# 16 bit comparisons on VectorE in a graph kernel: a 16 bit number table in PSUM, one-hots laid out number by number, selection matrices in two halves

## The chip, the cores and the metric

The kernel runs on 1 core of one Trainium2 chip. A core has five engines with queues of their own: TensorE (PE; its weight loads are listed apart as PEld), VectorE (DVE), ScalarE (ACT), GpSimd (POOL) and SyncE (SP), and 16 DMA engines. The metric is the device time in microseconds (us); of the kernel before, three runs were timed.

## What is computed

There are 12500 nodes with 64 numbers each and 212500 edges, sorted by their destination `dst`. Two graph layers follow each other, cut here to what matters:

```python
def _L0_gnn_ref(node_feats, edge_feats, src, dst, W1, b1, W2, b2, gamma, beta):
    msg = node_feats[src] + edge_feats
    agg = jax.ops.segment_sum(msg, dst, num_segments=n_nodes)
    h = jax.nn.relu(agg @ W1 + b1) @ W2 + b2
    ...                                   # batch norm over the nodes

def _L1_gnn_ref(x, edges, W1, b1, W2, b2, ln_w, ln_b):
    # two of: xw[src] * enorm[:, None], summed by dst, + b, relu; then one norm over everything
    ...
h = jnp.maximum(_layernorm(x), 0.0); x = x + _L0_gnn_ref(h, edge_attr_64, ...)
h = jnp.maximum(_layernorm(x), 0.0); x = x + _L1_gnn_ref(h, edge_index, ...)
```

So there are three passes over the edges (pass 0 for the first layer, passes 1 and 2 for the second), each a gather of rows by `src` and a sum by `dst`.

## The kernel before

A pass sums the edges in two ways. The edges of the lowest destinations are summed by **count matrices** ("dense windows"): for a window of 125 destinations, a matrix of 12500 sources by 125 destinations says how many edges lie between each pair, and TensorE multiplies it by the node table, in 100 matmuls of 125x125 times 125x193 (`app`, line 1110). Pass 0 has 54 such windows, passes 1 and 2 have 69. The rest of the edges come in **groups** of 1280 edges (128 partitions of NT=10 edges) and one small last group: POOL gathers the source rows from DRAM with one indirect DMA for each of the 10 edges of a partition (`pool_gather`, line 1273), and TensorE adds them up by destination with 10 matmuls whose weights are a **selection matrix** S, 128 edges by W=96 destinations, one for each of the 10 (`grp`, line 1132). In pass 0 all 167 groups also bring their edge features from DRAM; these take the same selection matrices (line 1125), and 79 of the groups are gathered besides. In passes 1 and 2 there are 54 gathered groups each.

The count matrices are themselves built on TensorE, in pass 0 for its 54 windows and in pass 1 for 17 more, and are kept in DRAM for the passes behind. One matrix takes 25 matmuls (`bld`, line 1089) of 128 edges each. Their weights are **one-hots** of a source's number within its block of 125 (VectorE, `ob`, line 958: five of them by one instruction of 5x125 elements, so NB4=5), and their moving operand is a one-hot of the block, times 1 or 256 for two destinations in one (VectorE, `oh`, line 961, 300 elements). ScalarE packs the counts out of PSUM (line 1211).

A one-hot is a comparison of a number with a row of numbers 0, 1, 2, ... Line 958 compares `modT` (16 bit) with `ps_i`, a table of 128 numbers in PSUM in fp32. Line 971 makes a whole selection matrix, 10x96 elements, by comparing `relT` (16 bit, edge's destination less the group's first) with the same table. Both results are 16 bit in SBUF, in rows of 125 or 96 destinations that lie side by side, and TensorE loads one such row in each partition as weights.

VectorE also splits the edge features of pass 0 into three bf16 parts (line 987, two subtractions of 650 fp32 elements per group, both inputs and the output in SBUF), folds the sums (lines 994, 1004) and adds them into `acc` (lines 1022, 1027).

The order of work on PE, ACT, DVE and SP is a list that `make_plan` writes: every item gets a due time in units of four `app` matmuls, and each engine runs its items by due time; a build's one-hots are due 3.3 units before its matmul, a group's S 7 units before its matmuls. The rings are short: NOH=6 `oh` buffers, NOB=3 `ob` buffers (15 one-hots), NS=2 selection matrices, NEDGE=2 buffers of edge features, NSLOT=4 groups of gathered rows. POOL runs the gathers in order, and a gather waits only until the group four before has been used. Before pass 0 stands a first part (layer norm, tables, the lists by run of edges), in which `dve_late_constants` (line 567) makes small constants.

Of the kernel before, what the change touches and what calls it, by code (L numbers as in the profile page):

```python
# [5 lines left out]
ALU = mybir.AluOpType  # L6
# [7 lines left out]
U8 = mybir.dt.uint8  # L14
# [3 lines left out]
P = 128  # L18
# [166 lines left out]
def bass_gnn_preln_kernel(nc, x, src, dst, edge, W01, b01, W02, b02, gamma, beta,  # L185
# [32 lines left out]
    with ExitStack() as ctx:  # L218
# [47 lines left out]
        relT = sb("relT", [P, NT, G], F16)  # L266
# [43 lines left out]
        ps_i = psum[:, 2, 0:P]  # L310
        ps_t = [psum[:, i, :] for i in range(2)]
# [34 lines left out]
        def sbuf(n):  # L346
            return part(o_S, n, NT * W // 2).bitcast(BF16).rearrange("p (t w) -> p t w", w=W)
# [165 lines left out]
        def sp_load():  # L513
            sp.dma_start(run_first, row_first).then_inc(l_first, 16)
            sp.dma_start(dst_i, dst_turned.rearrange("p t g -> p (t g)")).then_inc(l_dst, 16)
# [51 lines left out]
        def dve_late_constants():  # L567
# [4 lines left out]
            dve.tensor_copy(identb[:, :], ident[:, :]).then_inc(v_ident, 1)  # L572
            bound, late, limit = run_f[:, 0, :], run_f[:, 3, :], run_f[:, 2, :]
# [153 lines left out]
        def dve_lists():  # L727
            dve.wait_ge(l_dst, 2 * 16)
            firsts = base_b[:, 0:G].rearrange("p (a g) -> p a g", a=1).broadcast_to([P, NT, G])
            dve.tensor_tensor(relT[:, :, :], dst_i.rearrange("p (t g) -> p t g", g=G), firsts, ALU.subtract).then_inc(  # L730
                v_list, 1)
            dve.wait_ge(l_small, N_SMALL)
            V(dve.tensor_copy(rel_l[0:R, 0:2], dst_l[0:R, :]))
            V(dve.tensor_copy(rel_l[0:R, 4:5], dstb_l[0:R, :]))
            V(dve.tensor_scalar(rel_l[0:R, 2:4], rel_l[0:R, 0:2], rel_l[0:R, 4:5], None, ALU.subtract))
            dve.tensor_copy(relh_l[0:R, :], rel_l[0:R, 2:4]).then_inc(v_list, 1)

        def dve_check_lists():
            every = relT.rearrange("p t g -> p (t g)")
# [205 lines left out]
        def dve_pass(k, early=None):  # L945
            pl = plans[k]
            fe = FE if k == 0 else F
            for kind, v in half(pl, "dve", early):
                if kind == "oh":
                    if k == 1 and v == pl["b"]:  # L950
                        dve.wait_ge(st_x1, NCH * NBAND * 16)
                    if v % NB4 == 0:
# [10 lines left out]
                elif kind == "S":  # L963
# [4 lines left out]
                    if g < G:  # L968
                        rel = relT[:, :, g:g + 1].broadcast_to([P, NT, W])
                        it = ps_i[:, 0:W].rearrange("p (a w) -> p a w", a=1).broadcast_to([P, NT, W])  # L970
                        dve.scalar_tensor_tensor(out=S, in0=rel, scalar=0.0, in1=it, op0=ALU.add,  # L971
                                                 op1=ALU.is_equal).then_inc(v_S, 1)
                    else:
                        rel = relh_l[0:R, :].rearrange("p (t a) -> p t a", a=1).broadcast_to([R, 2, W])
                        it = ps_i[0:R, 0:W].rearrange("p (a w) -> p a w", a=1).broadcast_to([R, 2, W])
                        dve.scalar_tensor_tensor(out=S[0:R, 0:2, :], in0=rel, scalar=0.0, in1=it, op0=ALU.add,
                                                 op1=ALU.is_equal).then_inc(v_S, 1)
# [97 lines left out]
        def pe_pass(k, early=None):  # L1075
# [3 lines left out]
            for kind, v in half(pl, "pe", early):  # L1079
                if kind == "bld":  # L1080
# [8 lines left out]
                    pe.matmul(to[:, :, 2 * side:2 * side + 3], ob(v // NB4 % NOB)[:, v % NB4, :],  # L1089
# [24 lines left out]
                elif kind == "grp":  # L1114
# [7 lines left out]
                    if k == 0:  # L1122
                        pe.wait_ge(v_rest2, v + 1)
                        for t in range(nt):
                            last = pe.matmul(ps_q, S[0:parts, t, :], e3(v % NEDGE)[0:parts, t, :, :],  # L1125
                                             start=(t == 0), stop=(t == nt - 1 and not gathered))
                    if gathered:
# [3 lines left out]
                        for t in range(nt):  # L1131
                            last = pe.matmul(to, S[0:parts, t, :],  # L1132
# [252 lines left out]
        def slow_group(k, g, parts, nt):  # L1385
# [35 lines left out]
            gb, S = gbuf(0), sbuf(0)  # L1421
# [578 lines left out]
```

## Time and profile before

| | us |
|---|---|
| median of three runs | 2910.58 (2907.73 to 2920.95) |
| the profiled execution | 2908.32 |
| its span | 2906.8 |

Of the span PE is busy for 2552.8 us (88%), its weight loads for 2416.9 (83%), POOL for 1993.7 (69%), DVE for 1743.1 (60%) and ACT for 888.7 (31%). The granted clock of TensorE was 0.956 of full speed on the mean. "Busy" of PE counts from the start to the modelled end of matmuls that overlap, so it is no measure of how near PE is to its limit. The first part lasts to about 107 us, pass 0 to about 1337, the norms between the layers to about 1410, pass 1 to about 2180 and pass 2 to about 2900.

### The profile page before, as it was taken

The page shows a single profiled execution, that of the slowest core. Times are in us where ns is not written, and L with a number is a line of the kernel's source. Part 1 is how long each engine was busy: PE and PEld are TensorE (multiplying, and loading weights), DVE is VectorE, ACT ScalarE, POOL GpSimd, SP SyncE. Part 2 cuts the span into 40 slices and gives each one's busy share as a digit, 9 for nine tenths or more (in the row PEclk, how much of TensorE's full clock was granted, in tenths as well). Part 3 has the DMA queues.
Part 4 walks back from the last instruction along what each step waited for, and adds up shares of the span by engine and source line. Part 5 has one row for each costly group of instructions (what it writes and reads, how often), then busy time and mean ns, then how long its engine had stood idle before and what let it go on. Part 6 is the DMA issues. An engine that isn't in the chain of part 4 may idle for free.

```text
span 2906.8 us, 64340 instructions
## 1 busy us (share of the span) xinstructions
PE 2552.8 (88%) x25984; PEld 2416.9 (83%) x25984; DVE 1743.1 (60%) x4148; ACT 888.7 (31%) x1492; POOL 1993.7 (69%) x1903
## 2 busy tenths in 40 slices
PE   0388988989888898895699999999997999999996
PEld 0277878878787787784699999999997999999996
DVE  8898999989988899895444444454430222222222
ACT  7344444444444444454522222232210000000001
POOL 6777777777777778710377777767706777777772
PEclk9899999999999999996799999999998999999998
DMA  4455565555556555543765555655557666666664
GB/s 116 118 149 144 147 171 151 155 157 153 148 160 153 150 148 168 148 125 105 231 204 201 163 200 196 211 181 179 200 186 203 221 206 214 208 213 199 199 214 131
DMA packets 341214, 503.37 MB, mean 173 GB/s; under 512 B 278659, under 2 KB 284217, under 8 KB 316082
## 3 DMA queue, kind: packets, MB, share of 16 engines
q1 hardware_dynamic: 280102, 402.60, 42.8%
q0 software_dynamic: 60192, 93.34, 14.0%
q8 instruction: 214, 3.51, 0.5%
q10 hardware_dynamic: 616, 3.20, 0.4%
q14 instruction: 90, 0.73, 0.1%
HBM read 361.86 MB, written 137.13 MB: 172 GB/s over the span
## 4 chain that ended last, share of the span: by engine, by line
PE 42%; POOL 37%; issue 11%; DVE 5%; DMA 2%; ACT 1%; SPq 1%; DVEq 0%; ACTq 0%; POOLq 0%
POOL arena L1273 37%; PE psum L1110 32%; PE psum L1089 3%; PE psum L1132 3%; PE psum L1071 1%; DMA arena<-table,srcT 1%; ACT arena L818 1%; DMA arena<-in_edge_attr_dram 1%; SPq L1288 0%; PE psum L1125 0%; PE psum L1195 0%; DMA arena<-table 0%; DVE arena L961 0%; DVE arena L834 0%; DVE arena L844 0%
## 5 line engine op out<-in xcount | busy, mean ns | idle before, releaser
L1273 POOL DMA_INDIRECT arena<-table,srcT x1840 | 1913.0, 1040 | 696.3 <-issue 626.5
L1110 PE MATMUL psum<-arena 125*125 125x193 bf16 (+1 forms) x19200 | 2009.1, 250 | 44.8 <-DMA arena<-counts 23.0
L1110 PEld LDWEIGHTS psum<-arena 125*125 125x125 fp8e4 x19200 | 1879.1, 140 | 87.1 <-DMA arena<-counts 23.5
L1211 ACT CAST arena<-psum 125x500 uint16<-125x500 f32 (+1 forms) x923 | 647.3, 711 | 1084.3 <-PE psum L1089 1079.8
L1089 PE MATMUL psum<-arena 128*125 128x300 f16 x1775 | 609.9, 346 | 31.6 <-DVE arena L961 24.5
L961 DVE TENSOR_SCALAR arena<-iota,keyT,oddT 128x300 f16<-128x300 f16 x1775 | 579.3, 353 | 1.4 <-PE psum L1089 1.3
L1089 PEld LDWEIGHTS psum<-arena 128*125 128x125 f16 x1775 | 247.8, 140 | 79.5 <-DVE arena L961 58.4
L971 DVE SCALAR_TENSOR_TENSOR arena<-relT,psum 128x960 bf16<-128x960 f16 x272 | 308.6, 1134 | 0.0
L987 DVE TENSOR_TENSOR arena<-arena 128x650 f32<-128x650 f32 (+1 forms) x334 | 272.8, 817 | 24.8 <-DMA arena<-in_edge_attr_dram 24.6
L958 DVE TENSOR_TENSOR arena<-modT,psum 128x625 f16<-128x625 f16 x355 | 281.0, 792 | 0.2 <-issue 0.2
L994 DVE TENSOR_REDUCE arena<-psum 96x65 f32<-96x195 f32 (+1 forms) x275 | 96.3, 350 | 307.4 <-PE psum L1132 303.4
L1132 PE MATMUL psum<-arena 128*96 128x192 bf16 x1846 | 201.0, 258 | 59.2 <-DMA arena<-table,srcT 59.2
L1132 PEld LDWEIGHTS psum<-arena 128*96 128x96 bf16 x1846 | 174.9, 130 | 65.6 <-DMA arena<-table,srcT 54.8
L1255 ACT ACTIVATE cneg<-cst 125x1 f32<-125x1 f32 x25 | 5.1, 203 | 685.4 <-DVE arena L1046 685.4
L1004 DVE TENSOR_REDUCE arena<-psum 125x64 f32<-125x192 f32 x192 | 67.1, 349 | 234.0 <-PE psum L1110 233.8
L1125 PE MATMUL psum<-arena 128*96 128x195 bf16 (+1 forms) x1662 | 189.5, 262 | 2.4 <-DVE arena L987 2.4
L1022 DVE SCALAR_TENSOR_TENSOR acc<-psum,acc 65x96 f32 (+1 forms) x275 | 67.3, 245 | 194.4 <-PE psum L1191 161.1
L1125 PEld LDWEIGHTS psum<-arena 128*96 128x96 bf16 (+1 forms) x1662 | 166.6, 128 | 5.2 <-issue 3.9
L1027 DVE SCALAR_TENSOR_TENSOR acc<-psum,acc 64x125 f32<-64x125 f32 x192 | 53.3, 278 | 105.5 <-PE psum L1195 96.1
L1003 DVE COPY cnt<-psum 125x1 f32<-125x1 f32 x123 | 18.7, 152 | 154.3 <-PE psum L1110 153.9
L1643 POOL TENSOR_TENSOR arena<-arena 125x1600 f32<-125x1600 f32 x3 | 8.6, 2867 | 132.9 <-DVE arena L1633 132.9
L1191 PE MATMUL psum<-ident,arena 96*65 96x96 f32 (+1 forms) x275 | 70.5, 256 | 29.5 <-DVE acc L1027 27.1
(219 smaller groups left out, 954.2 us busy)
## 6 DMA issues: line engine op xcount, KB each, us to landing
arena<-counts SPq DMA_DIRECT2D x121, 1600.0 KB
counts<-arena SPq DMA_DIRECT2D x71, 1600.0 KB, 6.1
arena<-in_edge_attr_dram SPq DMA_DIRECT2D x166, 320.0 KB
arena<-table,srcT POOLq DMA_INDIRECT x1840
table<-arena SPq DMA_DIRECT2D x8, 1050.0 KB
table<-arena SPq DMA_DIRECT2D x25, 168.0 KB
arena<-table SPq DMA_DIRECT2D x4, 1050.0 KB
arena<-in_x_dram ACTq DMA_DIRECT2D x4, 700.0 KB
```

The source lines that it names most:

```text
L958: dve.tensor_tensor(ob(four % NOB), mod, it, ALU.is_equal)
L961: dve.tensor_scalar(oh(v % NOH), iota1[:, :], keyT[:, v:v + 1], oddT[:, v:v + 1], ALU.is_equal, ALU.mult).then_inc(v_oh, 1)
L971: dve.scalar_tensor_tensor(out=S, in0=rel, scalar=0.0, in1=it, op0=ALU.add, op1=ALU.is_equal).then_inc(v_S, 1)
L987: dve.tensor_tensor(ebuf(e, i + 1)[0:parts, 0:nt * FE], a, upper, ALU.subtract).then_inc(v_rest1 if i == 0 else v_rest2, 1)
L994: dve.tensor_reduce(qbuf(n % 2)[:, 0:fe], ps_q.rearrange("p (s f) -> p f s", s=3)[:, 0:fe, :], X, ALU.add).then_inc(v_fq, 1)
L1089: pe.matmul(to[:, :, 2 * side:2 * side + 3], ob(v // NB4 % NOB)[:, v % NB4, :], oh(v % NOH).rearrange("p (j m) -> p j m", m=3), start=(sid ...
L1110: last = pe.matmul(ps_v[n % 2][0:PN, 0:xc], A(slot)[0:PN, j, 0:PN], Xs[0:PN, j, 0:xc], start=(j == 0), stop=(j == J - 1))
L1125: last = pe.matmul(ps_q, S[0:parts, t, :], e3(v % NEDGE)[0:parts, t, :, :], start=(t == 0), stop=(t == nt - 1 and not gathered))
L1132: last = pe.matmul(to, S[0:parts, t, :], gbuf(slot)[0:parts, t, :].rearrange("p (s f) -> p s f", s=3), start=(k > 0 and t == 0), stop=(t = ...
L1191: pe.transpose(ps_g[0:fe, 0:W], qbuf(m % 2)[:, 0:fe], ident[0:W, 0:W]).then_inc(p_win, 1)
L1211: act.copy(A2(slot)[0:PN, :, i // 2 * NWORD:i // 2 * NWORD + n_w], ps_b[at % NBANK][0:PN, :].rearrange("p (j x) -> p j x", x=NWORD)[:, :, ...
L1273: pool.indirect_dma_start(out=gbuf(slot)[0:parts, t, :], out_offset=None, in_=tables[k], in_offset=bass.IndirectOffsetOnAxis(ap=idx, axis= ...
```

## The change

What it does:

- `num_dn` is a new table in PSUM, in fp16: element (d, n) holds d, for d from 0 to 124 and n from 0 to 4, so each number stands five times side by side. It is written once, by three new instructions in `dve_late_constants`: a memset of 313 words, a cast of 625 elements from the fp32 `iota`, and a copy of the 313 words into PSUM.
- Line 958's instruction stays one `tensor_tensor` of 625 elements. Its inputs are now `modT` (rows of 5 numbers, read again for each d) and `num_dn`, and its output lies as (d, n), so all three operands are 16 bit with a step of one element in the innermost dimension, where before `modT` stood still for 125 elements and the table was fp32.
- Line 971's one `scalar_tensor_tensor` of 960 elements becomes two `tensor_tensor` of 480 elements, for the edges 0 to 4 and 5 to 9 of each partition. S lies as (w, t); `relT` is turned to (g, t) for it, and with it the list that the host lays out.
- TensorE's weights are therefore no longer side by side: a one-hot of `ob` is read in steps of 5 elements (10 bytes), a selection matrix of S in steps of 10 elements (20 bytes). The matmuls, their number and sizes stay.

```diff
+        n_num = (PN * NB4 + 1) // 2
+        ps_n5 = psum[:, 2, P:P + n_num]
+        num_dn = ps_n5.bitcast(F16)[:, 0:PN * NB4].rearrange("p (d n) -> p d n", n=NB4)
...
         def ob(k):
 
-            return part(o_ob, k, n_ob).bitcast(F16)[:, 0:NB4 * PN].rearrange("p (n d) -> p n d", d=PN)
+            return part(o_ob, k, n_ob).bitcast(F16)[:, 0:NB4 * PN].rearrange("p (d n) -> p d n", n=NB4)
...
         def sbuf(n):
+            return part(o_S, n, NT * W // 2).bitcast(BF16).rearrange("p (w t) -> p w t", t=NT)
...
             dve.tensor_copy(identb[:, :], ident[:, :]).then_inc(v_ident, 1)
+            nums = arena[:, o_t + NE + 16:o_t + NE + 16 + n_num]
+            V(dve.memset(nums, 0.0))
+            V(dve.tensor_copy(nums.bitcast(F16)[:, 0:PN * NB4].rearrange("p (d n) -> p d n", n=NB4),
+                              iota[:, 0:PN].rearrange("p (d a) -> p d a", a=1).broadcast_to([P, PN, NB4])))
+            V(dve.tensor_copy(ps_n5, nums))
...
-                        mod = modT[:, v:v + NB4].rearrange("p (n a) -> p n a", a=1).broadcast_to([P, NB4, PN])
-                        it = ps_i[:, 0:PN].rearrange("p (a d) -> p a d", a=1).broadcast_to([P, NB4, PN])
-                        dve.tensor_tensor(ob(four % NOB), mod, it, ALU.is_equal)
+                        mod = modT[:, v:v + NB4].rearrange("p (a n) -> p a n", a=1).broadcast_to([P, PN, NB4])
+                        dve.tensor_tensor(ob(four % NOB), mod, num_dn, ALU.is_equal)
...
-                        rel = relT[:, :, g:g + 1].broadcast_to([P, NT, W])
-                        it = ps_i[:, 0:W].rearrange("p (a w) -> p a w", a=1).broadcast_to([P, NT, W])
-                        dve.scalar_tensor_tensor(out=S, in0=rel, scalar=0.0, in1=it, op0=ALU.add,
-                                                 op1=ALU.is_equal).then_inc(v_S, 1)
+                        for t0 in (0, NB4):
+                            rel = relT[:, g:g + 1, t0:t0 + NB4].broadcast_to([P, W, NB4])
+                            last = dve.tensor_tensor(S[:, :, t0:t0 + NB4], rel, num_dn[:, 0:W, :], ALU.is_equal)
+                        last.then_inc(v_S, 1)
...
-                    pe.matmul(to[:, :, 2 * side:2 * side + 3], ob(v // NB4 % NOB)[:, v % NB4, :],
+                    pe.matmul(to[:, :, 2 * side:2 * side + 3], ob(v // NB4 % NOB)[:, :, v % NB4],
...
-                            last = pe.matmul(ps_q, S[0:parts, t, :], e3(v % NEDGE)[0:parts, t, :, :],
+                            last = pe.matmul(ps_q, S[0:parts, :, t], e3(v % NEDGE)[0:parts, t, :, :],
...
-                            last = pe.matmul(to, S[0:parts, t, :],
+                            last = pe.matmul(to, S[0:parts, :, t],
```

The instructions' order stays on PE, ACT, POOL and SP. On DVE two places differ. The first is in the first part of the program, behind the constants (L572 writes the bf16 identity, L574 and L575 start the bounds of the edge runs); before and after:

```order
L571 TENSOR_SCALAR ident<-arena,rowf 128x128
L572 CAST identb<-ident 128x128
L574 TENSOR_SCALAR arena<-arena 128x14
L575 SCALAR_TENSOR_TENSOR arena<-arena 128x14
L577 TENSOR_SCALAR arena<-arena 128x14
```

```order
L577 TENSOR_SCALAR ident<-arena,rowf 128x128
L578 CAST identb<-ident 128x128
L580 MEMSET arena 128x313
L581 CAST arena<-arena 128x625
L583 COPY psum<-arena 128x313
L585 TENSOR_SCALAR arena<-arena 128x14
L586 SCALAR_TENSOR_TENSOR arena<-arena 128x14
L588 TENSOR_SCALAR arena<-arena 128x14
```

Three instructions have come in ahead of the bounds. The second place stands for every group, here one in pass 0, on DVE again; the lines are 958 and 968 for `ob`, 961 and 971 for `oh`, 971 and 981 for S, 987 and 995 for the edge features, before and after:

```order
L958 TENSOR_TENSOR arena<-modT,psum 128x625
L961 TENSOR_SCALAR arena<-iota,keyT,oddT 128x300
L1003 COPY cnt<-psum 125x1
L1004 TENSOR_REDUCE arena<-psum 125x64
L971 SCALAR_TENSOR_TENSOR arena<-relT,psum 128x960
L961 TENSOR_SCALAR arena<-iota,keyT,oddT 128x300
L994 TENSOR_REDUCE arena<-psum 96x65
L961 TENSOR_SCALAR arena<-iota,keyT,oddT 128x300
L987 TENSOR_TENSOR arena<-arena 128x650
```

```order
L968 TENSOR_TENSOR arena<-modT,psum 128x625
L971 TENSOR_SCALAR arena<-iota,keyT,oddT 128x300
L1011 COPY cnt<-psum 125x1
L1012 TENSOR_REDUCE arena<-psum 125x64
L981 TENSOR_TENSOR arena<-relT,psum 128x96x5 x2
L971 TENSOR_SCALAR arena<-iota,keyT,oddT 128x300
L1002 TENSOR_REDUCE arena<-psum 96x65
L971 TENSOR_SCALAR arena<-iota,keyT,oddT 128x300
L995 TENSOR_TENSOR arena<-arena 128x650
```

The selection matrix has become two instructions in the same place; nothing else has moved.

## Rows read from the trace of the kernel before

**Rows 1.** The page: chain of waits by engine, then by line, shares of the span.

```profile
PE 42%; POOL 37%; issue 11%; DVE 5%; DMA 2%; ACT 1%; SPq 1%; DVEq 0%; ACTq 0%; POOLq 0%
```

**Rows 2.** Busy time by stretch: PE, PEld, DVE, ACT, POOL, then clock, DMA.

```profile
110.00:1250.00 1140.00, 1000.60 (x8889) 899.07 (x8887) 1029.15 (x2456) 506.38 (x792) 900.69 (x780) 0.95 0.57 153
1255.00:1337.00 82.00, 71.47 (x591) 59.30 (x588) 60.62 (x147) 32.21 (x58) 0.00 (x0) 0.90 0.52 140
1420.00:2170.00 750.00, 747.48 (x8211) 736.69 (x8210) 341.79 (x947) 204.35 (x309) 513.30 (x532) 1.00 0.58 197
2210.00:2900.00 690.00, 663.41 (x7706) 659.23 (x7704) 151.09 (x366) 27.21 (x81) 488.66 (x518) 0.98 0.61 201
```

**Rows 3.** POOL's groups in pass 0: count, busy us, mean ns, idle before.

```profile
L1273 POOL DMA_INDIRECT arena<-table,srcT x778 | 898.9, 1155 | 237.1 <-issue 236.2 <-PE psum L1125 0.6 <-PE psum L1132 0.3
```

**Rows 4.** The same of POOL in pass 2, 2210 to 2900 us.

```profile
L1273 POOL DMA_INDIRECT arena<-table,srcT x516 | 486.9, 944 | 157.3 <-issue 157.0 <-PE psum L1132 0.3
```

**Rows 5.** DVE's and PE's groups in pass 0, 110 to 1250 us.

```profile
L961 DVE TENSOR_SCALAR arena<-iota,keyT,oddT 128x300 f16<-128x300 f16 x1278 | 418.0, 353 | 1.4 <-PE psum L1089 1.3
L987 DVE TENSOR_TENSOR arena<-arena 128x650 f32<-128x650 f32 x310 | 254.1, 820 | 21.6 <-DMA arena<-in_edge_attr_dram 21.6
L958 DVE TENSOR_TENSOR arena<-modT,psum 128x625 f16<-128x625 f16 x256 | 202.6, 791 | 0.0
L971 DVE SCALAR_TENSOR_TENSOR arena<-relT,psum 128x960 bf16<-128x960 f16 x156 | 176.7, 1133 | 0.0
...
L1089 PE MATMUL psum<-arena 128*125 128x300 f16 x1278 | 443.3, 349 | 27.3 <-DVE arena L961 20.4 <-ACT arena L1211 4.0 <-issue 0.2
L1132 PE MATMUL psum<-arena 128*96 128x192 bf16 x780 | 90.6, 269 | 49.8 <-DMA arena<-table,srcT 49.8
```

**Rows 6.** The timeline of POOL and DVE: start us, length us, what.

```profile
616.79 0.82 DVE L987 TENSOR_TENSOR arena<-arena 128x650 f32<-128x650 f32 x1
616.82 1.61 POOL L1273 DMA_INDIRECT arena<-table,srcT  x1 [0.30 <-issue]
617.80 0.82 DVE L987 TENSOR_TENSOR arena<-arena 128x650 f32<-128x650 f32 x1
...
621.03 1.14 DVE L971 SCALAR_TENSOR_TENSOR arena<-relT,psum 128x960 bf16<-128x960 f16 x1
621.70 0.94 POOL L1273 DMA_INDIRECT arena<-table,srcT  x1 [0.30 <-issue]
622.10 0.35 DVE L961 TENSOR_SCALAR arena<-iota,keyT,oddT 128x300 f16<-128x300 f16 x1
```

**Rows 7.** The chain in order of time, pieces: start us, us, what.

```profile
18.27 0.18 DVE arena L575
106.84 1.05 POOL arena L1273
1241.52 0.92 PE psum L1125 x10
1248.03 0.85 PE psum L1132 x10
1509.76 5.11 PE psum L1110 x60
1515.65 0.85 PE psum L1071 x8
```

**Rows 8.** The last gather of pass 0, and a 16 bit DVE operation, in the timeline.

```profile
1247.18 0.89 POOL L1273 DMA_INDIRECT arena<-table,src_l  x1 [0.30 <-issue]
...
15.52 2.00 DVE L602 TENSOR_SCALAR arena<-arena 128x1792 bf16<-128x1792 f16 x3
```

**Rows 9.** DVE's and PE's groups in the tail of pass 0, 1255 to 1337 us.

```profile
L971 DVE SCALAR_TENSOR_TENSOR arena<-relT,psum 128x960 bf16<-128x960 f16 x10 | 11.4, 1140 | 0.0
L958 DVE TENSOR_TENSOR arena<-modT,psum 128x625 f16<-128x625 f16 x12 | 9.5, 792 | 0.0
L1145 PE MATMUL psum<-acc,w 64*128 64x500 f32 x8 | 5.3, 753 | 4.0 <-DVE acc L1022 4.0
```

More of the change, by code:

```diff
@@ L13 @@
 U16 = mybir.dt.uint16
-U8 = mybir.dt.uint8
 X = mybir.AxisListType.X
@@ L265, in bass_gnn_preln_kernel @@
         srcT = sb("srcT", [P, NT, G - G0], I32)
-        relT = sb("relT", [P, NT, G], F16)
+        relT = sb("relT", [P, G, NT], F16)
         keyT = sb("keyT", [P, NBLD + NBLD % 2], F16)
@@ L310, in bass_gnn_preln_kernel @@
         ps_i = psum[:, 2, 0:P]
+        n_num = (PN * NB4 + 1) // 2
+        ps_n5 = psum[:, 2, P:P + n_num]
+        num_dn = ps_n5.bitcast(F16)[:, 0:PN * NB4].rearrange("p (d n) -> p d n", n=NB4)
+        assert NT == 2 * NB4
         ps_t = [psum[:, i, :] for i in range(2)]
@@ L346, in sbuf, with sbuf_rows @@
         def sbuf(n):
+            return part(o_S, n, NT * W // 2).bitcast(BF16).rearrange("p (w t) -> p w t", t=NT)
+        def sbuf_rows(n):
             return part(o_S, n, NT * W // 2).bitcast(BF16).rearrange("p (t w) -> p t w", w=W)
@@ L514, in sp_load @@
             sp.dma_start(run_first, row_first).then_inc(l_first, 16)
-            sp.dma_start(dst_i, dst_turned.rearrange("p t g -> p (t g)")).then_inc(l_dst, 16)
+            sp.dma_start(dst_i, dst_turned.rearrange("p g t -> p (g t)")).then_inc(l_dst, 16)
             sp.dma_start(base_b, group_first.broadcast_to([P, NG])).then_inc(l_dst, 16)
@@ L728, in dve_lists @@
             dve.wait_ge(l_dst, 2 * 16)
-            firsts = base_b[:, 0:G].rearrange("p (a g) -> p a g", a=1).broadcast_to([P, NT, G])
-            dve.tensor_tensor(relT[:, :, :], dst_i.rearrange("p (t g) -> p t g", g=G), firsts, ALU.subtract).then_inc(
+            firsts = base_b[:, 0:G].rearrange("p (g a) -> p g a", a=1).broadcast_to([P, G, NT])
+            dve.tensor_tensor(relT[:, :, :], dst_i.rearrange("p (g t) -> p g t", t=NT), firsts, ALU.subtract).then_inc(
                 v_list, 1)
@@ L738, in dve_check_lists @@
         def dve_check_lists():
-            every = relT.rearrange("p t g -> p (t g)")
+            every = relT.rearrange("p g t -> p (g t)")
             dve.wait_ge(v_list, 2)
@@ L968, in dve_pass @@
                     if g < G:
-                        rel = relT[:, :, g:g + 1].broadcast_to([P, NT, W])
-                        it = ps_i[:, 0:W].rearrange("p (a w) -> p a w", a=1).broadcast_to([P, NT, W])
-                        dve.scalar_tensor_tensor(out=S, in0=rel, scalar=0.0, in1=it, op0=ALU.add,
-                                                 op1=ALU.is_equal).then_inc(v_S, 1)
-                    else:
[L974 to L977, printed above, removed]
+                        for t0 in (0, NB4):
+                            rel = relT[:, g:g + 1, t0:t0 + NB4].broadcast_to([P, W, NB4])
+                            last = dve.tensor_tensor(S[:, :, t0:t0 + NB4], rel, num_dn[:, 0:W, :], ALU.is_equal)
+                        last.then_inc(v_S, 1)
+                    else:
+                        rel = relh_l[0:R, :].rearrange("p (a t) -> p a t", a=1).broadcast_to([R, W, 2])
+                        dve.tensor_tensor(S[0:R, :, 0:2], rel, num_dn[0:R, 0:W, 0:2], ALU.is_equal).then_inc(v_S, 1)
                 elif kind in ("rest1", "rest2"):
@@ L1420, in slow_group @@
             pool.sem_clear(t_idx)
-            gb, S = gbuf(0), sbuf(0)
+            gb, S = gbuf(0), sbuf_rows(0)
             for t in range(nt):
@@ L1982 @@
     laid['x'] = x.reshape(-1, PN, F).transpose(1, 0, 2).reshape(PN, -1)
-    for name, a in (('src_turned', src), ('dst_turned', dst)):
-        laid[name] = a[0:n_groups * P * NT].reshape(n_groups, P, NT).transpose(1, 2, 0)
+    for name, a, order in (('src_turned', src, (1, 2, 0)), ('dst_turned', dst, (1, 0, 2))):
+        laid[name] = a[0:n_groups * P * NT].reshape(n_groups, P, NT).transpose(*order)
     behind = _np.stack([_np.full(P, n_nodes, dst.dtype), _np.zeros(P, dst.dtype)], axis=1)
```

## The prediction, before the changed kernel ran

> **What bounds the kernel now.** The change touches VectorE (DVE) and the layout of TensorE's (PE's) weights, so I first ask who sets the end in each stage. The page's chain of waits gives PE 42%, POOL 37% and DVE 5% [rows 1]. The table by stretch says where [rows 2]. From 110 to 1250 us (pass 0) three engines look full: DVE 1029 of 1140 us, PE 1001, POOL 901. In pass 1 (1420 to 2170) PE is busy for 747 of 750 us and DVE for 342; in pass 2 (2210 to 2900) PE for 663 of 690, DVE for 151. So passes 1 and 2 are PE's, and no saving on DVE can shorten them.
>
> In pass 0 the busy share misleads. POOL's group has 237.1 us of idle time in front of 778 gathers, and 236.2 of it is "issue", 0.30 us ahead of each; for the matmuls that free its four slots it waits 0.9 us in all [rows 3]. POOL thus starts each gather as soon as the one before has ended, without a break: from 106.84 to 1247.18 + 0.89 = 1248.1 us [rows 7, 8] is 1141 us for 782 gathers, 1.46 us each. As it never waits for DVE or PE, a faster DVE gives it nothing. The others show the other side: PE waits 49.8 us for gathered rows and 27.3 us ahead of line 1089, of which 20.4 for one-hots [rows 5]. DVE is the second slowest; it falls behind and catches up within the four groups that the slots allow.
>
> Can DVE slow POOL in another way? A gather takes 1155 ns on the mean in pass 0 and 944 in pass 2 [rows 3, 4], so 778 x 0.211 = 164 us of pass 0 is stretch. The timeline says with which DVE work: the gather at 616.82 takes 1.61 us beside two of line 987 (fp32, both inputs in SBUF, 0.82 us each), the one at 621.70, whose first half lies beside line 971, takes 0.94 [rows 6]. Those that stretch it are line 987 and, less, line 961; the change touches neither, and their number stays.
>
> **The change part by part.**
>
> *Line 958, 355 instructions (270 for pass 0, 85 for pass 1).* 625 elements take 791 ns, line 971's 960 take 1133 [rows 5]: (1133 - 791) / 335 = 1.02 ns per element, and 0.15 us fixed, of which 0.07 lies beside the next instruction (971 starts at 621.03, is 1.14 long, the next starts at 622.10 [rows 6]). The trace has no two-input 16 bit operation with all operands packed. Bounds: 1.04 ns per element as now; from below line 602's one-input 16 bit operation, 3 of 1792 elements in 2.00 us [rows 8], some 0.35 ns. I take half of the present rate, 0.52 ns: two numbers a step is what 16 bits beside 32 suggests, and line 961 (300 elements in 353 ns, (0.353 - 0.15) / 300 = 0.68 [rows 5]) lies between. Saved: 625 x 0.5 = 0.32 us each.
>
> *Line 971, 272 instructions (166 for pass 0).* Now 1.06 us from start to start; then 2 x (0.07 + 480 x 0.52) = 0.64, so 0.43 us saved. At the present rate it would be 2 x (0.07 + 0.50) = 1.14, 0.08 more.
>
> DVE's work in pass 0 falls by 270 x 0.32 + 166 x 0.43 = 158 us (bounds: 13 more; 208 less), in pass 1 by 50 and in pass 2 by 23. In pass 0 nothing of it reaches the end while POOL runs: it becomes DVE waiting for gathers. Value 0, bounds -15 to +15 us, for the stretch of the gathers may shift as DVE's gaps do.
>
> At this place the Trainium skill disagrees with itself. Its page "VectorE: DVE Perf Modes" (the perf-mode tier table) gives `tensor_tensor` one element per cycle as soon as an operand is in PSUM; "Vector Engine (DVE) Microarchitecture Reference" (5.1, performance modes) lets it take two with one source in PSUM, also for rows of odd length such as these 5. No row here decides it. By the first DVE saves nothing, by the second what I took; the sum is the same but for the tail.
>
> *The tail of pass 0, 1255 to 1337 us.* POOL is idle there and DVE is busy for 61 of 82 us, PE for 71 [rows 2]. DVE has 10 of line 971 and 12 of line 958 in it [rows 9]: 10 x 0.43 + 12 x 0.32 = 8.1 us saved. PE is nearly full, so only its gaps can close: 82 - 71.5 = 10.5 us, of which 4.0 wait for sums that DVE adds [rows 9], and some for DMA. Value -5, bounds -8 to 0.
>
> *The head.* Three DVE instructions come in on the chain, which runs through line 575 at 18.27 us [rows 7]. The memset and the copy have 313 elements, the cast 625; at 1.02 ns and 0.15 fixed, each waiting for the one before: 0.47 + 0.79 + 0.47 = 1.7; at half the rate 1.1. Value +1.5, and the first gather at 106.84 goes with it.
>
> *The weight loads.* This is where the change can cost. All loads of the trace read columns side by side. An `app` matmul with its load takes 5.11 / 60 = 85 ns, a selection matmul 0.85 / 10 = 85 [rows 7]: 192 or 193 columns set this, the loads hide behind them. How long may a load take before it shows? Line 1071 loads 125 four-byte columns and moves only 64: 0.85 / 8 = 106 ns a pair [rows 7], so the load sets it, at 0.85 ns per column. If a strided 2-byte column is no slower than that four-byte one, a selection matrix (96 columns) takes 82 ns: hidden. A one-hot (125 columns) takes 106, 21 more than the matmul ahead: 425 in pass 1, 9 us at most; its step of 10 bytes is the smaller one, so I take 3. Bounds 0 and, if a strided column takes twice a four-byte one (1.7 ns), the rival below.
>
> *Nothing else.* relT, its copy from DRAM and its subtraction keep their sizes; no queue gets another DMA and no engine another wait.
>
> **Sum** against the profiled execution (2908.3; its span is 2906.8): +1.5 - 5 + 3 = -0.5. The runs' median lies 2.3 above that execution, so the forecast is 2910 in terms of the median, own range 2896 to 2924: no change that a measurement tells (about 0.5%, 15 us).
>
> **The rivals.**
>
> *A, slower: strided weights load slower than the matmul ahead.* For it: the load is barely hidden (82 of 85 ns even at the four-byte rate), and moving columns that step by 4 bytes (line 1125) already take 0.92 per 10 against 0.85 [rows 7], 3 columns more but 7 ns, not 1. Against: those 7 ns are little. It decides from 85 ns a load, 0.85 ns per column. At 1.7 ns a selection load takes 163 ns, +78 for each: in passes 1 and 2, where PE has no slack, 1064 x 78 = 83 us, and 425 one-hots with, say, +60 make 26. In pass 0, 2440 x 78 + 1350 x 60 = 271 us against PE's idle 1140 - 1001 = 139 [rows 2]: +132. Together +241, 3150 us; at 1.05 ns per column, (101 - 85) x 1064 and 46 x 425 make +37 with pass 0 absorbed, 2947.
> The Trainium skill names such a mechanism: "SBUF — State Buffer" (specifications, and its note on cachelines) says that SBUF is read in 16-byte lines, that full rate needs at least two hits in a line, and that each access that crosses to a new line pays. It gives no figure. In S every column would be in another line, in `ob` five of eight. No load here has such a step; line 1125's four columns to a line, nearly at full rate, do not contradict it.
>
> *B, faster: gathers stretch less.* If DVE is no longer full, gaps fall between lines 987 and 961, and POOL gets in. Against: the stretch goes with the count of those two. A quarter of 164 us gone gives 2869.
>
> *C, faster: DVE is the bound of pass 0 after all.* Its waits on PE and full 1029 us speak for it, POOL's 0.9 us against. All 158 us off, until PE's 1001 us stop it: -139, 2771.
>
> *D, the 16 bit rate does not come.* DVE +13 us in pass 0, hidden; 10 x 0.08 us in the tail instead of -5: 2916, no change.
>
> **How the numbers follow.** The forecast 0.43, D 0.09, A 0.26 (a third of it near 2947, the rest above 2960), B 0.16, C 0.04, and 0.02 for what I don't see. Faster: B, C and a little of the forecast, 0.22; slower: A and a little of the forecast, 0.28; within 0.5%: 0.50. The range for 8 in 10 reaches over most of B and the cheap part of A: 2872 to 2965; above it is the dear part of A.
>
> **What would show it.** Right: line 968 at about 475 ns and line 981 at about 400; POOL's issue still without waits in pass 0, 1.46 us per gather; PE's waits for gathered rows grown from 49.8 us to over 100; `app` and selection matmuls still 85 ns a pair in pass 2; the first gather 1 to 2 us later. Wrong: selection matmuls at 100 ns or more a pair in passes 1 and 2 (A); gathers of pass 0 under 1100 ns on the mean (B); POOL's last gather of pass 0 long before 1240 us (B or C); lines 968 and 981 at 790 and 650 ns (D).

## The result, and the profile after

The changed kernel takes 3090.35 us (median of four runs, 3087.82 to 3091.70); the kernel before, timed again beside it, 2914.76 (2907.73 to 2920.95). The ratio is 1.0602, with a 95% interval of 1.0573 to 1.0631: 175.6 us, or 6%, slower. I had forecast 2910 and a range up to 2965. Rival A, the strided weight loads, is what happened; the range reached only over its cheap part.

The page's chain of waits of the changed kernel, by engine, shares of the span, beside [rows 1]:

```profile
PE 84%; DVE 6%; DMA 4%; ACT 2%; issue 1%; SPq 1%; POOL 1%; DVEq 1%; ACTq 0%; POOLq 0%
```

POOL has fallen from 37% to 1% and PE has doubled. The stretches of the changed kernel that answer to [rows 2], with the same columns (us, PE, PEld, DVE, ACT, POOL, granted clock, DMA share, GB/s):

```profile
110.00:1290.00 1180.00, 1144.19 (x8547) 1069.79 (x8548) 924.59 (x2520) 491.12 (x761) 856.22 (x780) 0.99 0.54 144
1300.00:1420.00 120.00, 117.01 (x894) 106.51 (x894) 87.62 (x241) 46.45 (x78) 0.00 (x0) 0.99 0.46 134
1510.00:2330.00 820.00, 818.10 (x8263) 807.45 (x8260) 316.24 (x1003) 204.86 (x309) 511.48 (x531) 1.00 0.54 180
2350.00:3060.00 710.00, 697.49 (x7665) 694.70 (x7666) 138.79 (x397) 18.49 (x69) 499.23 (x530) 0.99 0.62 198
```

In pass 0 PE now has 36 us without work where it had 139, and its granted clock is 0.99 where it was 0.95: it has few pauses left. The reader's first sign of the cause is that PE does the same 25,984 matmuls in more time. The groups of weight loads over the whole span, their forms apart (count, busy us, mean ns, idle before), of the kernel before:

```profile
L1089 PEld LDWEIGHTS psum<-arena 128*125 128x125 f16 x1775 | 247.8, 140 | 79.5 <-DVE arena L961 58.4 <-issue 18.9
L1132 PEld LDWEIGHTS psum<-arena 128*96 128x96 bf16 x1840 | 174.4, 130 | 65.3 <-DMA arena<-table,srcT 54.8 <-issue 10.3
```

and of the changed kernel:

```profile
L1097 PEld LDWEIGHTS psum<-arena 128*125 128x125 f16 x1775 | 391.8, 221 | 49.5 <-DVE arena L971 31.7 <-issue 17.2
L1140 PEld LDWEIGHTS psum<-arena 128*96 128x96 bf16 x1840 | 323.1, 260 | 9.4 <-DMA arena<-table,srcT 9.4
```

A selection matrix's load has gone from 130 to 260 ns and a one-hot's from 140 to 221, with the same columns and bytes. The chain of the changed kernel in pass 0 (start us, us, what) shows what that does to a pair of load and matmul; it answers to [rows 7]:

```profile
606.38 1.68 PE psum L1133 x10
608.06 1.67 PE psum L1140 x10
```

That is 167 to 168 ns a pair, where before it was 85 (line 1132) and 92 (line 1125). From start to start of the records, a one-hot's pair (line 1097, which moves 300 elements) takes 211 ns for 156.

POOL in pass 0 of the changed kernel answers to [rows 3], and PE's two groups to [rows 5]:

```profile
L1281 POOL DMA_INDIRECT arena<-table,srcT x779 | 854.9, 1097 | 320.0 <-issue 222.5 <-PE psum L1140 97.5
```

```profile
L1097 PE MATMUL psum<-arena 128*125 128x300 f16 x1232 | 483.2, 395 | 11.9 <-DVE arena L971 8.8 <-ACT arena L1219 0.5
L1140 PE MATMUL psum<-arena 128*96 128x192 bf16 x750 | 137.5, 333 | 9.0 <-DMA arena<-table,srcT 9.0
```

The roles are swapped. POOL waits 97.5 us for PE to free its slots (0.9 before), and PE waits 9.0 us for gathered rows (49.8 before) and 11.9 ahead of the one-hot matmuls (27.3 before). The mean gather of 1097 ns is under the 1100 that I had named as a sign of rival B; here it stands in a slower kernel, so that sign was no good by itself.

**Where the time is.** Between the two medians lie 175.6 us, between the spans of the two traces 182.5. The stages, from the start of their first to the start of their last instruction, in us:

| | before | after | difference |
|---|---|---|---|
| first gather of pass 0 | 106.8 | 108.8 | +1.9 |
| pass 0, first gather to the norms | 1234.8 | 1321.5 | +86.7 |
| pass 1, first to last `app` matmul | 765.4 | 831.4 | +66.0 |
| pass 2, first to last `app` matmul | 698.4 | 725.6 | +27.2 |

The differences add to 182 of the 182.5 us. In pass 1 they are the loads and nothing else: 532 selection pairs x 82 ns and 425 one-hots x 55 ns make 67. In pass 0, 782 pairs of line 1140 x 82, 1662 of line 1133 x 76 and 1350 one-hots x 55 are 265 us more work for PE, of which 178 did not lengthen the pass. Of the 87 that did, 42 lie before POOL's last gather (1183 us of gathers for 1141) and 45 behind it (139 us for 94), where PE works off what it is late with. In pass 2, 532 x 82 = 44 gave 27.

**VectorE.** Not all comparisons got as fast as expected. The changed kernel's groups over the whole span, forms apart:

```profile
L981 DVE TENSOR_TENSOR arena<-relT,psum 128x480 bf16<-128x480 f16 x544 | 298.6, 633 | 0.0
L968 DVE TENSOR_TENSOR arena<-modT,psum 128x625 f16<-128x625 f16 x355 | 189.3, 533 | 0.1
```

A block of one-hots went from 791 to 533 ns (I took 475), but each half of a selection matrix took 633 (I took 400). With 0.15 us fixed that is 0.61 ns per element for the first and 1.00, the old rate, for the second. VectorE's busy time from the first gather to the norms fell from 1099 to 1026 us, by 73 where I had 158.

### The profile page after: what moved, and what is told of

Read it like the earlier page. It is cut to its first block, busy times and chain, and to the rows that moved or that the text cites. A ratio compares the mean times of both kernels' runs of the same rounds, so it can differ in the third digit from the quotient of the medians.

```text
span 3089.3 us, 64615 instructions
## 1 busy us (share of the span) xinstructions
PE 2853.4 (92%) x25984; PEld 2744.4 (89%) x25984; DVE 1641.6 (53%) x4423; ACT 891.2 (29%) x1492; POOL 1945.9 (63%) x1903
## 4 chain that ended last, share of the span: by engine, by line
PE 84%; DVE 6%; DMA 4%; ACT 2%; issue 1%; SPq 1%; POOL 1%; DVEq 1%; ACTq 0%; POOLq 0%
PE psum L1118 49%; PE psum L1097 11%; PE psum L1140 10%; PE psum L1133 8%; DMA arena<-in_edge_attr_dram 3%; PE psum L1079 1%; DVE arena L995 1%; PE psum L1153 1%; PE psum L1156 1%; PE psum L1199 1%; PE psum L1203 1%; DVE arena L971 1%; POOL arena L1281 1%; ACT arena L829 1%; DVEq L1028 0%
## 5 line engine op out<-in xcount | busy, mean ns | idle before, releaser
L1281 POOL DMA_INDIRECT arena<-table,srcT x1840 | 1867.3, 1015 | 843.7 <-issue 610.0
L1097 PE MATMUL psum<-arena 128*125 128x300 f16 x1775 | 695.1, 394 | 12.2 <-DVE arena L971 8.8
L1097 PEld LDWEIGHTS psum<-arena 128*125 128x125 f16 x1775 | 391.8, 221 | 49.5 <-DVE arena L971 31.7
L1140 PE MATMUL psum<-arena 128*96 128x192 bf16 x1846 | 338.1, 332 | 9.0 <-DMA arena<-table,srcT 9.0
L1140 PEld LDWEIGHTS psum<-arena 128*96 128x96 bf16 x1846 | 324.4, 260 | 9.7 <-DMA arena<-table,srcT 9.4
L1133 PE MATMUL psum<-arena 128*96 128x195 bf16 (+1 forms) x1662 | 304.3, 330 | 0.3 <-DVE arena L995 0.3
L981 DVE TENSOR_TENSOR arena<-relT,psum 128x480 bf16<-128x480 f16 x544 | 298.6, 633 | 0.0
L1133 PEld LDWEIGHTS psum<-arena 128*96 128x96 bf16 (+1 forms) x1662 | 292.2, 260 | 1.4 <-issue 1.2
L968 DVE TENSOR_TENSOR arena<-modT,psum 128x625 f16<-128x625 f16 x355 | 189.3, 533 | 0.1
```

The source lines that it names most:

```text
L968: dve.tensor_tensor(ob(four % NOB), mod, num_dn, ALU.is_equal)
L981: last = dve.tensor_tensor(S[:, :, t0:t0 + NB4], rel, num_dn[:, 0:W, :], ALU.is_equal)
L1133: last = pe.matmul(ps_q, S[0:parts, :, t], e3(v % NEDGE)[0:parts, t, :, :], start=(t == 0), stop=(t == nt - 1 and not gathered))
L1140: last = pe.matmul(to, S[0:parts, :, t], gbuf(slot)[0:parts, t, :].rearrange("p (s f) -> p s f", s=3), start=(k > 0 and t == 0), stop=(t = ...
L1281: pool.indirect_dma_start(out=gbuf(slot)[0:parts, t, :], out_offset=None, in_=tables[k], in_offset=bass.IndirectOffsetOnAxis(ap=idx, axis= ...
```

## The experiments

Each kernel was timed in three rounds beside the kernel before on the same chip, unless it says otherwise. Diffs are against the changed kernel where not told, and each shows only the lines that matter.

**One part alone: one-hots changed, selection matrices as before.**

```diff
-                    S = sbuf(n % NS)
+                    S = sbuf_rows(n % NS)
-                            last = pe.matmul(to, S[0:parts, :, t],
+                            last = pe.matmul(to, S[0:parts, t, :],
```

(and S written by one `scalar_tensor_tensor` again).

> The changed kernel with its selection matrices as before: one instruction, one row of 96 destinations per edge, read side by side; one-hots stay 16 bit and strided (10 bytes). Theory L (strided weight loads set the time; in the changed kernel's trace a selection matmul with its load takes 167 ns for 85, a one-hot's matmul 211 for 156): only 1775 x 55 = 98 us of TensorE work is left, 425 of them (23 us) in pass 1 without slack, 74 us in pass 0 against 139 us of idle, most of it absorbed; 2940 to 2955 us. Theory D (the time comes from VectorE: new reads of PSUM, two instructions for a selection matrix, later results): the half of the cost that belongs to the selection matrices goes too, but the matmul pairs stay slow; 3000 or so.

2915.29 us (2908.14 to 2919.56), ratio 0.9998, interval 0.9983 to 1.0014: no change, below what I expected. Pass 1 is 22 us longer (787.5 for 765.4, 425 x 55 = 23), and the gathers of pass 0 are 13 us shorter (1128.4 for 1141.2, 1139 ns on the mean for 1155). So in pass 1 the strided one-hots cost what the arithmetic says, and the shorter gathers of pass 0 give about as much back.

**The other part alone: selection matrices changed, one-hots as before.**

```diff
-                        dve.tensor_tensor(ob(four % NOB), mod, num_dn, ALU.is_equal)
+                        it = ps_i[:, 0:PN].rearrange("p (a d) -> p a d", a=1).broadcast_to([P, NB4, PN])
+                        dve.tensor_tensor(ob(four % NOB), mod, it, ALU.is_equal)
-                    pe.matmul(to[:, :, 2 * side:2 * side + 3], ob(v // NB4 % NOB)[:, :, v % NB4],
+                    pe.matmul(to[:, :, 2 * side:2 * side + 3], ob(v // NB4 % NOB)[:, v % NB4, :],
```

> The changed kernel with its one-hots (line 958 of before) as before; selection matrices stay in two halves and strided by 20 bytes. Theory L: 1064 x 82 = 87 us in passes 1 and 2, and in pass 0 1662 x 76 + 782 x 82 = 190 us against 139 of idle, +51 or a little more; 3050 to 3070 us. With e1 the two parts should add up to more than the whole in passes 1 and 2 alone, and to less than it in pass 0, where each can use the idle time by itself. Theory D: as e1, 3000 or so.

3033.34 us (3028.65 to 3037.94), ratio 1.0404, interval 1.0366 to 1.0441, or +120 us. That is below the 3050 to 3070 expected; the selection matrices are still the larger part. Alone the two cost 2 and 120, together 176. Pass 1 adds up: +22 and +43 alone, +66 together. Pass 0, from the first gather on, does not: -14 and +52 alone, +87 together. Each alone can use PE's pauses; together they have used them up.

**The strides alone: VectorE slow as before, its results laid out as after.**

```diff
-                        dve.tensor_tensor(ob(four % NOB), mod, num_dn, ALU.is_equal)
+                        it = ps_i[:, 0:PN].rearrange("p (d a) -> p d a", a=1).broadcast_to([P, PN, NB4])
+                        dve.tensor_tensor(ob(four % NOB), mod, it, ALU.is_equal)
```

(S likewise, by one `scalar_tensor_tensor` of 960 elements.)

> Only the layout: results laid out and loaded as in the changed kernel, but compared with the fp32 table, one instruction for a selection matrix, so VectorE is as slow as before (about 790 and 1130 ns). Theory L: TensorE has all of its loss, 3090 us, and up to 30 more if VectorE, again busy for some 90% of pass 0, makes TensorE wait there as well. Theory D: VectorE as before, so the time of before, 2915.

3096.56 us (3094.90 to 3098.35), ratio 1.0622, interval 1.0586 to 1.0658. The strides alone bring the whole loss. The faster VectorE, which this kernel lacks, is worth 6 us at most in their presence: the two intervals overlap, so the 6 us are not told from nothing.

**VectorE's part alone: VectorE as after, TensorE reads side by side.** The weights then hold other numbers than S and `ob` mean, so the sums differ, and the kernel's own comparison of its counts (line 1070) is made to hold always.

```diff
-                            last = pe.matmul(to, S[0:parts, :, t],
+                            last = pe.matmul(to, S[0:parts, t, :],
```

> Only VectorE's part: VectorE's instructions as in the changed kernel, but TensorE reads its weights side by side at the old places (so the weights are other numbers, and the result isn't the reference's; the check on the sum of counts is set to pass). Theory L together with the forecast's claim that POOL's gathers set pass 0: VectorE's 130 us of saved work give nothing but the tail, 2900 to 2915 us. If VectorE was the bound of pass 0 (rival C of the prediction): 2780 to 2830. Theory D: 3090, as the changed kernel.

The one-hots of line 1097 are read side by side too. 2889.81 us (2888.37 to 2891.07), ratio 0.9910, interval 0.9876 to 0.9944: 24 us faster, 10 below the lower end expected. The gathers' stretch is 1124.0 us for 1141.2, and POOL's row shows how (110 to 1233 us):

```profile
L1281 POOL DMA_INDIRECT arena<-table,srcT x779 | 882.5, 1133 | 237.4 <-issue 237.1 <-PE psum L1140 0.3
```

POOL still hardly waits for a slot (0.3 us); each gather is 22 ns shorter, which makes the 17 us. That is rival B in small. Rival C, 2780 to 2830 here, is refuted. The tail, for which I had forecast -5, is unchanged (93.6 us from the last gather to the norms, as before).

**How long is a load at each step?** The kernel before, with each of a group's ten selection matrices read in another step, from 1 to 10 elements (2 to 20 bytes) over the same buffer; the sums differ. One run, no rounds.

```diff
+            flat = S.rearrange("p t w -> p (t w)")
+            return flat[0:parts, 0:(W - 1) * (t + 1) + 1:t + 1]
-                            last = pe.matmul(to, S[0:parts, t, :],
+                            last = pe.matmul(to, S_step(S, parts, t),
```

> The kernel before, but the ten selection matmuls of a group read their 96 weight columns in steps of 1, 2, ... 10 elements (2 to 20 bytes) out of the same matrix (other weights, so the result isn't the reference's). By lines, time of a pair = 96 x 1.67 x min(1, bytes / 16) + 7, at least 85: 85 ns up to 6 bytes, 87 at 8, 107 at 10, 127 at 12, 147 at 14, 167 from 16 on. If it were a threshold: 85 below some step and 167 above it, with nothing between. If each step cost in proportion beyond 16 bytes too: over 167 at 18 and 20.

The run took 2945.64 us. The timeline of weight loads of one group of pass 2 (start us, length us), in order of steps of 2, 4, ... 20 bytes:

```profile
2412.01 0.12 PEld L1138 LDWEIGHTS psum<-arena 128*96 128x96 bf16 x1
2412.10 0.12 PEld L1138 LDWEIGHTS psum<-arena 128*96 128x96 bf16 x1
2412.18 0.14 PEld L1138 LDWEIGHTS psum<-arena 128*96 128x96 bf16 x1
2412.27 0.17 PEld L1138 LDWEIGHTS psum<-arena 128*96 128x96 bf16 x1
2412.36 0.19 PEld L1138 LDWEIGHTS psum<-arena 128*96 128x96 bf16 x1
2412.45 0.23 PEld L1138 LDWEIGHTS psum<-arena 128*96 128x96 bf16 x1
2412.59 0.25 PEld L1138 LDWEIGHTS psum<-arena 128*96 128x96 bf16 x1
2412.74 0.27 PEld L1138 LDWEIGHTS psum<-arena 128*96 128x96 bf16 x1
2412.92 0.27 PEld L1138 LDWEIGHTS psum<-arena 128*96 128x96 bf16 x1
2413.09 0.26 PEld L1138 LDWEIGHTS psum<-arena 128*96 128x96 bf16 x1
```

Medians over all groups are 123, 125, 144, 166, 193, 232, 252, 272, 268 and 264 ns. The load grows from a step of 6 bytes to one of 16 and is flat from there. At 16 bytes each column lies in another 16 bytes; 20 bytes make it no worse. What a pair costs is the time from the start of a matmul to that of the next. Its medians in pass 2 are 85 ns at each step up to 8 bytes, then 112, 135, 155, 175, 172 and 167: the matmul's 192 columns hide a load up to 8 bytes of step.

My sum of 1.67 ns per 16-byte line opened and 7 ns more was fitted to the 167 ns at 20 bytes alone; it gave 107, 127, 147 and 167 for 10 to 16 bytes and is 5 to 8 ns low there. The growth with each step up to 16 bytes and the flat end refute a bare threshold and a cost that goes on with the distance. In pass 1 these times make 53 groups x 0.41 = 22 us, and the pass is 22 us longer. For a one-hot the same sum gives 78 lines and 137 ns, an estimate; an `app` matmul (86 ns from start to start) stands ahead of it, so some 51 ns would show, and 55 did.

The Trainium skill's "SBUF — State Buffer" (note on cachelines) has the unit of 16 bytes right; that two hits in a line are enough is not borne out, since a step of 8 bytes has two and its load takes 166 ns for 123. Here that excess hides behind the matmul.

**A step of 10 bytes for S: two blocks of five side by side.**

```diff
+            return part(o_S, n, NT * W // 2).bitcast(BF16).rearrange("p (h w t) -> p h w t", h=2, t=NB4)
-                            last = dve.tensor_tensor(S[:, :, t0:t0 + NB4], rel, num_dn[:, 0:W, :], ALU.is_equal)
+                            last = dve.tensor_tensor(S[:, h, :, :], rel, num_dn[:, 0:W, :], ALU.is_equal)
```

> The changed kernel with the two halves of a selection matrix as blocks of their own, so both write side by side and TensorE's columns step by 10 bytes, not 20; one-hots as changed. By lines: five of eight columns open a line, 96 x 1.67 x 5/8 + 7 = 107 ns a pair. Passes 1 and 2 lose 1064 x 22 + 425 x 55 = 47 us less some idle, pass 0 absorbs its part; 2915 to 2935 us. If a step is only slow or not slow, from 10 bytes on: 167 ns and 3085 us. VectorE's halves: if their mean of 633 ns came from the rows of five with a gap behind each, they fall to about 400; if 16 bit comparisons don't run faster with rows of five from relT, they stay over 600.

2932.54 us (2930.67 to 2935.64), ratio 1.0069, interval 1.0046 to 1.0092. The selection pairs take 112 ns in pass 2 (1.12 us for ten in the chain), for 107 by the sum, and the write has changed too (this kernel's group, whole span):

```profile
L985 DVE TENSOR_TENSOR arena<-relT,psum 128x480 bf16<-128x480 f16 x544 | 216.1, 436 | 0.0
```

436 ns for 633. The same 480 elements, of the same inputs, run at 0.60 ns each when the rows of five that are written touch, and at 1.00 when a gap of five lies between them. Where in a word the rows begin is not the reason: in the changed kernel the half whose rows all begin at a multiple of four bytes takes 612 ns on the mean, the other 655.

In pass 0 the gathers of this kernel take 1105.0 us for 1141.2, but the stretch from the last of them to pass 1 is 28 us longer. In pass 2 its selection pairs cost 532 x 27 ns = 14 us more, and the pass is no longer than before (696.5 us for 698.4).

**A step of 4 bytes for S: five blocks of pairs, one instruction.** The one-hots are as before; the table is of pairs.

```diff
+            return part(o_S, n, NT * W // 2).bitcast(BF16).rearrange("p (h w t) -> p h w t", h=NT // 2, t=2)
+                        rel = relT[:, g, :].rearrange("p (h a t) -> p h a t", a=1, t=2).broadcast_to([P, NT // 2, W, 2])
+                        num = num_d2[:, 0:W, :].rearrange("p (b w) t -> p b w t", b=1).broadcast_to([P, NT // 2, W, 2])
+                        dve.tensor_tensor(S, rel, num, ALU.is_equal).then_inc(v_S, 1)
-                            last = pe.matmul(to, S[0:parts, :, t],
+                            last = pe.matmul(to, S[0:parts, t // 2, :, t % 2],
```

> Selection matrices in five side-by-side blocks of two edges, made by one 16 bit instruction of 960 elements (table with each number twice), so TensorE's columns step by 4 bytes; one-hots as before. Theory L by lines (a strided column costs 1.67 ns when it opens a 16 byte line; 96 x 1.67 + 7 is the 167 ns of the changed kernel): four columns share a line, 0.42 ns each, so a selection matmul stays at 85 ns. VectorE: 960 x 0.52 + 0.15, some 650 ns for 1133. As POOL's gathers stretch a little less beside a VectorE with more gaps (the run with VectorE's part alone showed 1133 for 1155 ns on the mean), 2895 to 2905 us. A theory that any step above 2 bytes is slow: a pair over 85 ns and over 2950 us.

2898.88 us (2893.51 to 2904.74), ratio 0.9956, interval 0.9937 to 0.9976: the loss is gone and a small gain left. Passes 1 and 2 last 765.4 and 695.1 us (before 765.4 and 698.4). The shorter gathers that I expected from it did not come. POOL's row of this kernel (110 to 1248 us):

```profile
L1284 POOL DMA_INDIRECT arena<-table,srcT x779 | 899.9, 1155 | 237.4 <-issue 236.5 <-PE psum L1136 0.6 <-PE psum L1143 0.3
```

VectorE is busy for 78 us less in pass 0 (1021 for 1099), and a gather takes 1155 ns as before. So less work on VectorE does not by itself shorten the gathers.

**Both in pairs.** As the last, and the one-hots ten at a time in five blocks of pairs (NB4=10, NOB=2).

```diff
-                        dve.tensor_tensor(ob(four % NOB), mod, num_dn, ALU.is_equal)
+                        mod = modT[:, v:v + NB4].rearrange("p (h a n) -> p h a n", a=1, n=2).broadcast_to([P, NB4 // 2, PN, 2])
+                        num = num_d2.rearrange("p (b d) n -> p b d n", b=1).broadcast_to([P, NB4 // 2, PN, 2])
+                        dve.tensor_tensor(ob(four % NOB), mod, num, ALU.is_equal)
-                    pe.matmul(to[:, :, 2 * side:2 * side + 3], ob(v // NB4 % NOB)[:, :, v % NB4],
+                    pe.matmul(to[:, :, 2 * side:2 * side + 3], ob(v // NB4 % NOB)[:, v % NB4 // 2, :, v % 2],
```

> As e5, and one-hots of sources also in pairs: ten by one instruction (five blocks of 125 x 2, two buffers of ten instead of three of five), TensorE's columns in steps of 4 bytes. All matmul pairs as before (85 and 156 ns), VectorE 1250 x 0.52 + 0.15 = 800 ns for ten one-hots instead of 2 x 791. VectorE saves some 170 us in pass 0, nearly twice what the changed kernel saves; POOL still sets pass 0, so the gain is what the gathers' stretch gives back: 2875 to 2895 us. If VectorE's time counted by itself, 2780.

2875.92 us (2872.85 to 2881.34), ratio 0.9883, interval 0.9858 to 0.9908. This kernel beats both. Its VectorE groups over the whole span, and one group of weight loads:

```profile
L986 DVE TENSOR_TENSOR arena<-relT,psum 128x960 bf16<-128x960 f16 x272 | 173.0, 636 | 0.0
L972 DVE TENSOR_TENSOR arena<-modT,psum 128x1250 f16<-128x1250 f16 x178 | 140.7, 791 | 0.2
```

```profile
L1144 PEld LDWEIGHTS psum<-arena 128*96 128x96 bf16 x1840 | 171.6, 129 | 83.3 <-DMA arena<-table,srcT 71.5 <-issue 11.6
```

Ten one-hots now cost what five did, 791 ns, a selection matrix 636 for 1133, and a load 129 ns as before. And yet 497 ns x 166 and 396 ns x 270, 189 us of VectorE's work in pass 0 (its busy time there fell by 164, from 1099 to 935), bring 37 us. POOL's row of this kernel (110 to 1220 us) tells why:

```profile
L1285 POOL DMA_INDIRECT arena<-table,srcT x779 | 871.6, 1119 | 237.4 <-issue 236.5 <-PE psum L1137 0.6 <-PE psum L1144 0.3
```

POOL still runs all but without a wait (0.9 us), at 1119 ns for 1155.

**Does POOL set pass 0?** Half of pass 0's gathers are left out, and each gathered row serves two edges; against the kernel before, and the same cut in the kernel with both in pairs:

```diff
-            for t in range(nt):
+            for t in range(nt // 2 if k == 0 else nt):
-                                             gbuf(slot)[0:parts, t, :].rearrange("p (s f) -> p s f", s=3),
+                                             gbuf(slot)[0:parts, t // 2 if k == 0 else t, :].rearrange("p (s f) -> p s f", s=3),
```

> The run with half of POOL's gathers of pass 0 left out once more, since on the chip of the last one the kernel before itself took 4191 us. POOL the bound of pass 0: 2805 to 2875 us against some 2913 of the kernel before. VectorE the bound (rival C): 2905 to 2915.

> The same cut in the version with pairs, once more for the same reason. POOL the bound of pass 0: 2725 to 2775 us, so that VectorE's saved work is worth 80 us or more with half of the gathers, against 37 with all of them. VectorE the bound all along: 37 in both.

Cut from the kernel before: 2854.28 us (2843.03 to 2856.80), ratio 0.9792, interval 0.9756 to 0.9828, -55 us. Cut from the pairs: 2782.74 (2781.26 to 2786.99), ratio 0.9561, interval 0.9532 to 0.9590, which is 93 below the pairs with all gathers and a little above the 2775 that I gave as its upper end. The sums of both differ from the reference's, since half of the rows are missing. POOL's group of the first (110 to 1180 us):

```profile
L1273 POOL DMA_INDIRECT arena<-table,srcT x388 | 475.7, 1226 | 560.9 <-PE psum L1132 464.0 <-issue 96.9
```

Now POOL waits 464 us for its slots and is no bound; VectorE is the fullest engine, 1008 of these 1070 us. VectorE's saving is worth 72 us between these two kernels (80 or more expected) and 37 with all gathers: half of what it could bring was held back by POOL. The same two kernels had first run on a chip on which even the kernel before took 4191 us, with issue waits all over the trace (3836 us for the first, 3795 for the second); nothing is concluded from that.

## Why the prediction was wrong

*The step that failed* is "The weight loads": "If a strided 2-byte column is no slower than that four-byte one ... hidden", and from it "I take 3". The term came out at 376 us more work on PE (265 in pass 0, 67 in pass 1, 44 in pass 2), of which 180 reached the end, where 3 stood. I had priced a strided column by line 1071's four-byte columns. Those lie side by side, four to 16 bytes; the columns of S are 20 bytes apart, each in another 16. The run with the strides alone (+183 us) and the one with steps of 2 to 20 bytes (a pair 85 to 175 ns) show that this distance is the cause. The nearest row was not near in what mattered, the distance from one column to the next. The bound that I did name, 1.7 ns per column, was very close for S (167 ns a pair, 163 forecast); the one-hots cost +55, +60 forecast. Both were luck: 1.7 was twice the four-byte rate and +60 a round number, and no row stood behind either. From those Rival A gave +241; its pass-1 part and its work for pass 0 (271 for 265) held. What it had too large is what reaches the end: pass 0 +87 for +132, pass 2 +27 for 42.

*"In passes 1 and 2, where PE has no slack."* True of pass 1 (67 us worked out, 66 measured). In pass 2 only 27 of 44 came through. [Rows 4] make 644 us of POOL in the 690 (486.9 + 157.3): a gather each 1.25 us, without a pause. PE's wait for them in pass 2, before:

```profile
PE psum L1132 <- DMA arena<-table,srcT: 9.4, 6, 3.4
```

In the changed kernel this wait is gone, and PE's granted clock is 0.985 on the mean of the pass for 0.975, some 6 us more; together that is about the 17 that did not come through. The gathers of pass 2 take 664 us from first to last in both kernels, and all of the loss lies behind the last one (55 us for 27). So pass 2 had about 16 us of slack, and other runs agree: the steps of 2 to 20 bytes added 22 us of pairs and 6 us of time, the two blocks 14 and none. That it was close to POOL's pace I read out of the rows only afterwards; no run took its gathers away.

*The slack of pass 0.* I set PE's idle time at 139 us. It absorbed 178, and the granted clock went from 0.949 to 0.985. From the first gather to the norms, PE's time without work fell from 157 to 47 us, and the time by which the clock fell short of full speed from 63 (1235 x 0.051) to 20 (1322 x 0.015): 110 and 43 us. That is a rough split, since a pause at the lower clock counts in both, and 25 us are in neither.

*VectorE's rate.* The half rate came for the one-hots in part (533 ns for 475, against 791) and not for S (633 for 400): a row of five took 3.1 ns where five elements in rows of two took 2.6, and when it was written with a gap behind it 5.0, as if no two elements went together. Rival D was right for S alone. The Trainium skill's "VectorE: DVE Perf Modes" (tier table) allows one element per cycle with any operand in PSUM; 0.51 ns per element (636 ns for 960, 791 for 1250) contradicts it. The Trainium skill's "Vector Engine (DVE) Microarchitecture Reference" (5.1) has the rate right, but not the odd rows of this case: its pairs that run on from one row into the next would give five the rate of two, and 0.61 was measured.

*POOL sets pass 0.* Held for the kernel before: a faster VectorE alone left POOL without waits and took 17 us off its stretch, through shorter gathers, which is a little past my lower bound of -15. Which of VectorE's instructions stretch the gathers stays open. VectorE's busy time in pass 0 and the mean gather do not go together: 1099 us and 1155 ns before, 1021 and 1155 with S in pairs, 1013 and 1133 with VectorE's part alone, 989 and 1109 with two blocks, 935 and 1119 with both in pairs. That it is lines 987 and 961 was not tried by itself. The sign that I had named for being right, PE's waits for gathered rows over 100 us, did not come either where VectorE was faster and the loads were not: 56.2 us with VectorE's part alone.

*The head*: +1.5 forecast, the first gather came 1.9 later; the three instructions take 1.72 us in the chain (18.17 to 19.89). *The tail*: -5 forecast; +45 in the changed kernel, through PE; 0 with VectorE's part alone and -6 with both in pairs.

## What to carry to other kernels

Before a layout is turned to suit one engine, price every reader of it: 16 bit comparisons ran at up to twice the rate here, and the loads of their results took twice as long on the engine that was nearer to its limit. A stride is priced by the distance between elements, not by their size: here a weight load stayed hidden up to a step of 8 bytes and cost 82 ns each at 20. Two numbers side by side were enough for the best rate seen on VectorE, so the narrowest interleaving that gives the rate (pairs) is the one to take.

## What the runs showed of the hardware

- A weight load of 96 two-byte columns takes 123 ns side by side, 125 in steps of 4 bytes, 166 at 8 bytes, 272 at 16 and no more beyond. With a matmul of 192 columns a pair takes 85 ns up to 8 bytes, 112 at 10 and 167 to 175 from 16 on (1.7 to 1.9 ns per 16-byte line opened).
- VectorE's 16 bit `tensor_tensor` with one operand in PSUM runs at 0.51 ns per element in rows of two, 0.60 in touching rows of five, 1.00 when rows of five are written with gaps between them.
- An indirect gather takes 0.94 us and 0.30 of issue in pass 2, where VectorE is busy for 151 of 690 us. In pass 0, with VectorE much fuller, its mean was 1109 to 1155 ns, all but without a wait between the two engines; it did not simply follow VectorE's busy time.
